# Sin evaluation of half of the weight tiles moved from the output stage into the scan loop, in groups of four

## The reference

```python
xn = _layernorm(x, axis=-1)
x = x + attn(xn, ...) + ffn(xn, ...)
...
# attn: a selective scan, D_MODEL = 1024 channels, D_STATE = 16 states
delta = softplus(xn @ Wd.T + bd)
a_pos = softplus(a_log) + 0.0001
state = exp(-delta_t * a_pos) * state + delta_t * b_param * x_t
y_t = state.sum(-1)
attn = y @ Wo.T + bo
...
# ffn
real = xn @ cos(theta + theta_noise)
imag = xn @ sin(phi + phi_noise)
ffn = sqrt(real * real + imag * imag)
```

## Time and profile before

| what | us |
|---|---|
| median of 2 runs | 1127.46 (1127.39 to 1127.54) |
| profiled execution, slowest core | 1126.65 |
| its span (core 3) | 1124.9 |
| spans of the eight cores | 1118.1 to 1124.9 |
| DVE busy | 815.5 |
| ACT busy | 581.6 |
| PE busy | 582.7 |
| POOL busy | 156.3 |

### The profile page before, as it was taken

How to read it: one execution, slowest core, us unless ns; L and a number is a source line. 1 busy time by engine, 2 the same in 40 slices (tenths; PEclk the granted TensorE clock), 3 DMA queues, 4 the chain that set the end, 5 groups by cost and what they waited for, 6 DMA issues and landing times.

```text
span 1124.9 us, 9382 instructions; the slowest of 8 cores (1118.1 to 1124.9 us)
## 1 busy us (share of the span) xinstructions
PE 582.7 (52%) x2248; PEld 240.0 (21%) x2248; DVE 815.5 (72%) x725; ACT 581.6 (52%) x923; POOL 156.3 (14%) x132
## 2 busy tenths in 40 slices
PE   0423334445456654555544556665555554455685
PEld 0301011112113331222211113333222211121353
DVE  3359988889833349989899984334889899998423
ACT  4574666665573225556555553322456555655430
POOL 2478000000011100000000002120000000000232
PEclk9955555556678866666655668886766656665799
DMA  8777101000011310000000001331100000000023
GB/s 229 196 217 210 62 19 29 28 19 1 1 47 57 116 42 0 1 1 0 1 1 1 0 0 48 87 113 56 43 1 0 0 1 1 0 0 1 28 71 112
DMA packets 36325, 51.66 MB, mean 46 GB/s; under 512 B 3120, under 2 KB 19760, under 8 KB 36272
## 3 DMA queue, kind: packets, MB, share of 16 engines
q1 hardware_dynamic: 33584, 42.68, 13.5%
q0 software_dynamic: 2688, 8.39, 2.2%
HBM read 42.67 MB, written 8.39 MB: 45 GB/s over the span
## 4 chain that ended last, share of the span: by engine, by line
DVE 42%; issue 23%; PE 20%; ACT 10%; POOL 2%; DMA 1%; DVEq 1%; ACTq 0%; POOLq 0%; SPq 0%
DVE grot L718 34%; PE pd L852 6%; PE pt L569 3%; PE pt L579 3%; ACT bdg_bf L171 3%; PE pd L278 3%; DVE sfm L866 2%; ACT abar L673 1%; DVE gcar L729 1%; DMA xsub<-xin 1%; PE pe L357 1%; DVEq L111 1%; POOL xsub L619 1%; PE py L880 1%; DVE xsub L419 1%
## 5 line engine op out<-in xcount | busy, mean ns | idle before, releaser
L718 DVE TENSOR_TENSOR_SCAN grot<-abar,gcar,vbuf 128x768 bf16<-128x768 f32 (+1 forms) x384 | 647.4, 1747 | 56.0 <-ACT abar L673 45.9
L673 ACT ACTIVATE abar<-delta,nega 128x768 f32<-128x768 f32 (+1 forms) x384 | 342.8, 898 | 281.2 <-DVE grot L718 278.4
L756 PE MATMUL pe<-grot,bdg_bf 128*128 128x384 bf16 x256 | 91.1, 457 | 125.7 <-DVE grot L718 125.7
L756 PE MATMUL py<-grot,bdg_bf 128*128 128x384 bf16 x256 | 88.4, 450 | 117.4 <-DVE grot L718 117.4
L278 PE MATMUL pd<-xnbf,wd_bf 128*128 128x384 bf16 (+1 forms) x368 | 99.2, 452 | 18.4 <-ACT xsub L297 15.0
L743 PE MATMUL py<-grot,bdg_bf 128*128 128x512 bf16 x64 | 33.5, 537 | 77.6 <-DVE grot L718 77.6
L619 POOL TENSOR_TENSOR xsub<-r,i 128x384 f32<-128x384 f32 (+1 forms) x9 | 18.1, 2011 | 398.0 <-ACT i L611 398.0
L852 PE MATMUL pd<-ybf,wo_bf 128*128 128x384 bf16 (+1 forms) x320 | 73.0, 378 | 0.0
L569 PE MATMUL pt<-xnbf,cos_bf 128*128 128x384 bf16 (+1 forms) x320 | 70.8, 370 | 0.7 <-ACT r L606 0.7
L743 PE MATMUL pe<-grot,bdg_bf 128*128 128x512 bf16 x64 | 34.3, 541 | 67.8 <-DVE grot L718 67.6
L278 PEld LDWEIGHTS pd<-xnbf,wd_bf 128*128 128x128 bf16 x368 | 49.7, 136 | 67.4 <-issue 58.7
(11 more groups left out here) (109 smaller groups left out, 560.5 us busy)
## 6 DMA issues: line engine op xcount, KB each, us to landing
xsub<-xin SPq DMA_DIRECT2D x14, 512.0 KB, 4.2
xres<-xin SPq DMA_DIRECT2D x32, 192.0 KB, 2.4
out<-osub POOLq DMA_DIRECT2D x32, 192.0 KB, 2.7
xres<-xin SPq DMA_DIRECT2D x8, 256.0 KB, 3.9
out<-osub POOLq DMA_DIRECT2D x8, 256.0 KB, 3.2
r<-wdt SPq DMA_DIRECT2D x6, 256.0 KB, 7.3
i<-wdt SPq DMA_DIRECT2D x6, 256.0 KB, 7.3
etmp<-tht SPq DMA_DIRECT2D x6, 256.0 KB, 5.2
```

Source lines behind the costliest of these rows:

```text
L673: sx = run("scalar", lambda e, sl=sl_ab, par=par, dt=dt, n=n, tp=tp: e.activation(out=abar[:, sl * TP:sl * TP + tp], in_=delta[:, par * TP ...
L718: vs = run("vector", lambda e, g=gsl, sl=sl_ab, par=par, dt=dt, n=n, tp=tp: e.tensor_tensor_scan(out=grot[:, g * TP:g * TP + tp], data0=ab ...
L756: td = run("tensor", lambda e, c=c, g=gsl, dt=dt, n=n, bb=ypair[c]: e.matmul(bb[:, 0:384], bdg_bf[:, (dt * NST + n) * P:(dt * NST + n + 1) ...
```

## The change

The Sin activations of h1_idx no longer stand in the output stage. They stand in the scan loop of phase 0 as four groups of four, one entry of `aux` at the end of the list in each of the passes 0, 1, 6 and 7, the passes that had no Sin group yet. The groups of passes 0 and 1 do the cosine tiles, those of passes 6 and 7 the sine tiles. They wait for POOL's additions as the others do, and set `trig_h1`.

```diff
                 if p == 0 and 2 <= dt < 6:
                     aux.append(("sinc", (dt - 2) * 4, 4))
+                if p == 0 and dt in (0, 1, 6, 7):
+                    q1 = {0: 0, 1: 1, 6: 2, 7: 3}[dt]
+                    aux.append(("sin1", q1 * 4, 4))
...
-                        elif kind == "sinc":
-                            idxs = h0_idx[adt:adt + ac]
+                        elif kind in ("sinc", "sin1"):
+                            idxs = (h0_idx if kind == "sinc" else h1_idx)[adt:adt + ac]
+                            ttrg = trig_s_last if kind == "sinc" else trig_h1
...
-                                trig_s_last[0] = run("scalar", lambda e, d=dst_, o=off_, ub=ub_: e.activation(
+                                ttrg[0] = run("scalar", lambda e, d=dst_, o=off_, ub=ub_: e.activation(
...
-                if p == 0 and it < 2:
-                    idxs = h1_idx[it * 8:it * 8 + 8]
-                    for t_ in idxs:
-                        (gsm_, g_ev_), _, _, _ = trig_cmds[t_]
-                        wait("scalar", gsm_, g_ev_)
-                    wait("scalar", "V", v_cv)
-                    for t_ in idxs:
-                        _, dst_, off_, ub_ = trig_cmds[t_]
-                        trig_h1[0] = run("scalar", lambda e, d=dst_, o=off_, ub=ub_: e.activation(
-                            out=d[:, o:o + 512], in_=d[:, o:o + 512], func=AF.Sin,
-                            bias=(cvals[:, 0:1] if ub else 0.0), scale=1.0), "S")
```

## The result

The changed kernel takes 1133.53 us in the median, before took 1127.18 in the same comparison; the ratio is 1.0058, with a 95% interval from 1.0046 to 1.0070. That is 6.5 us slower (5.2 to 7.9). The forecast was +4.7 us, and within 2%.

What follows compares the result with a forecast made beforehand. The prediction took DVE's scans as the largest chain share, 42%, with a chain over all engines ending last. Scan stalls added 13.0 us, the output stage gave back 8.3: net +4.7, forecast 1132.1 us, range 1127.5 to 1138.

Steps and rivals of the forecast that it cites:

- within 2%: Whole kernel: a time within 22.5 us of before, given 0.97, with slower 0.02 and faster 0.01.
- Stalls of the new groups: Scan loop: Sin groups delay DVE's scans by 0.5 us in pass 0, 4.6 in pass 1, 7.9 in passes 6 and 7.
- The cover in pass 0: Pass 0: scans slowed by POOL's additions, 2.49 us each, hide most of the cosine group, leaving 0.5 us delay.
- The chain of negmr: Output stage, first subtile: without Sin groups negmr's wait falls from 8.16 us to 0.79, a gain of 7.37.
- a collision with the output DMA: Output stage: output DMA may run into the subtile's load, taking 1 us off the lower bound of the gain.
- PE's rate at the transposes: First subtile: less PE idle time makes transposes faster, gaining 0.97 us from there to sfm; possibly nothing, or 2.2.
- The forecast's own range: Whole kernel: 1129.8 to 1139.2 us from the bounds of added and removed time.
- A: Output stage gives back all 14.4 us that ACT spends there, so 1126.1 us, not slower; chance 0.10.
- B: Stalls are paid but the output stage gives back nothing, as subtile load or slow PE replaces ACT; 1140.5 us; chance 0.09.
- C: Scan loop: each table switch costs more than its load because ACT must first finish; 5.1 us more, 1137.2; chance 0.07.
- D: Pass 0: the group waits for POOL's additions and starts 26.7 us later, giving 1158 us; chance 0.02.

Runs made afterwards that it cites:

- few_groups: Against before: loop Sin calls in two groups, eight h0 cosines in pass 0, sixteen sines in pass 2; h1 cosines stay in output stage; 1114.03 us, ratio 0.9894.
- no_h1: Against before: Sin activations of h1_idx left out altogether, so those tiles stay plain sums; 1117.83 us, ratio 0.9915.
- one_sin: The changed kernel with one Sin call instead of four in each of the four new groups; 1128.06 us, ratio 1.0019 to before.
- merged8: Against before: the sixteen h1 calls join the groups of passes 2 to 5, eight calls each, none in passes 0, 1, 6, 7; 1129.28 us, ratio 1.0014.
- pass7_late: The changed kernel with the sine group of pass 7 behind the abar of step 10 instead of step 2; 1133.55 us, ratio 1.0102 to before.
- pass6_late: The changed kernel with the sine group of pass 6 behind the abar of step 11 instead of step 6; 1130.67 us, ratio 1.0055 to before.

## Why the prediction was right, point by point

The sign and the mechanism came out, and the size within 1.8 us: +4.7 us forecast, +6.5 measured. The interval (5.2 to 7.9) leaves the forecast just outside, and the range of the prediction held the time. The main terms came from rows of the same work at another place and were met to some tenths, so it was not luck; the two that were off both concern PE's clock. By its steps:

- **Stalls of the new groups.** Passes 1, 6 and 7 as worked out from rows 2, 3, 12 and 13: 4.46, 3.85 and 3.84 us of idle time, passes 2 to 7 +7.7 against 7.9. Passes 0 and 1 became 4.5 us longer by the profile of before and 5.4 by the mean of the five kernels with the same program there (66.8), against 5.1 forecast.
- **The cover in pass 0.** Right in kind: few_groups put eight calls there for 1.8 us (68.6 against 66.8), where a group of eight in pass 2 stalls DVE for 6.67. Beside what the slow scans cover, the scans behind the stall are faster, which the prediction gave only as a bound.
- **The chain of negmr.** 7.37 forecast, 7.0 measured. Most of the difference lies in the rows: on core 3, which they show, the statistics of the subtile start 4.47 us behind the first sfm, and over the eight cores 4.72 (4.35 to 5.17). With the change it is 4.84 (4.26 to 5.82), so the load itself is 0.1 later. The prediction named a collision with the output DMA as a possible 1 us; no run told it apart from chance.
- **PE's rate at the transposes.** This term was mis-sized. I took 0.97 us, the idle time of PE then being 2.35 us and a little more. It was 3.57 on core 0, as the matmuls ahead start 0.8 earlier behind the first sfm and the statistics 0.4 later than on core 3 before, and the transposes stayed slow (1.09 us). Over the cores the stretch from negmr to the second sfm gained 0.6: in three it was 4.18, with transposes of 0.63, in five 5.5 to 6.8, with transposes of 1.09. The prediction took the rate from PE's idle time; in the runs it goes with the burst ahead of the first sfm and not with the idle time, so this term and the next may be one effect seen twice.
- **The step that was missing.** Nothing in the sum allowed for PE's matmuls ahead of the first sfm, which I let stand unchanged as they follow the scans. They cost 0.8 us more, at a place where before ACT's blocks would have covered it. With 0.4 at each of the two terms before, that is 1.6 of the 1.8 us between forecast and measurement, as far as the interval allows to say so.
- **Two slips in the bounds.** Twice 0.97 is 1.94 and not 2.2, and 4.6 for each of the four groups is 18.4 and not 18. The forecast's own range would be 1130.1 to 1139.6 instead of 1129.8 to 1139.2; the forecast does not hang on it. And 2% is not what this comparison can tell: its interval is 0.24% wide.
- **The rivals.** A, that all of ACT's 14.4 us comes back, is excluded by no_h1, whose output stage gave 7.8. B, that nothing comes back, by the wait of 0.79. C, that a switch costs more than its load: in pass 0 of the changed kernel abar, load, Sin calls, load and abar follow each other on ACT with gaps of at most 0.02 us, from 88.87 to 94.89, and one_sin leaves 1.8 us for a pair of loads in a stall, less than the 2.6 that they take, so there is no hidden part. That is also where the trace and the Trainium skill (ScalarE: Activation LUTs, "What ACT_TABLE_LOAD costs") part: with its drain, the pair would take 5.3 us. The advice of the Trainium skill (the same page, "Table sets: the hidden batching unit") to batch calls by set is borne out by merged8 and few_groups. D, a wait for POOL, did not occur: ACT idled 0.41 us before the abar of 88.87, for DVE, and the load followed at once.
- **What I had not seen.** That either half of the change alone is neutral, because the load of the subtile covers the cosine block whole and the sine block but for 2.0 us. The prediction charged both blocks to one wait and so gave their removal as one term; for the full change that was enough.

## What to carry to other kernels

Work that needs another activation table is not filler for a loop that lives on ACT: here each visit cost two loads of 1.28 us whatever it did, less some 0.8 us of slack. So make one visit with many calls, and put it where the loop is slow for another reason. Before taking work off an engine in a stretch, ask what else arrives late there: here a load that took 3.3 to 4.9 us to land, and the statistics behind it, hid one block of Sin calls, and removing the second block paid 0.1 or 2.0 us, where the first had paid 6.9 or 5.0. Moved work is best priced in both places by rows of the same kernel: the groups that were there already gave three of the four new stalls to within 0.2 us.

## What was not expected of the hardware

PE's clock at the start of a burst is not set by the idle time in front of it alone. The transposes of the first subtile took 1.09 us for four after 3.57 us of idle time on core 0 of the changed kernel, and a later subtile on the same core 1.09 after 3.10. On core 7 of the same execution those of the first subtile took 0.63 after 3.10 too. Over the runs, those of the first subtile were slow after as little as 2.89 us (one_sin, core 6) and fast after as much as 4.06 (one_sin, core 3). The two with 3.10, core 0 first:

```profile
365.36 1.09 PE L357 MATMUL pe<-csts,xsub 128*128 128x128 f32 x4 [3.10 <-DVE xsub L419]
```

```profile
342.65 0.63 PE L357 MATMUL pe<-csts,xsub 128*128 128x128 f32 x4 [3.10 <-DVE xsub L419]
```

With the matmuls behind them this is worth up to 2.6 us (4.18 against 6.75 from negmr to the second sfm), as much as some of the edits studied here, and it falls differently on the eight cores of one execution. What did sort the cores is the stretch to the first sfm, as told under pass7_late and pass6_late: core 0 has 8.7 us there, core 7 8.1. This spread is the reason to read stretches over all cores before a difference of a microsecond or two is given a cause.
